# Reading the scale of every softmax exponential from a column of SBUF instead of from a register of ScalarE

## The chip, the cores and the metric

The kernel runs on one core of a Trainium2 chip. The metric is the device time of one execution in microseconds (us); lower is better. PE is TensorE, ACT is ScalarE, DVE is VectorE, POOL is GpSimd and SP is SyncE. SBUF is the on-chip memory with 128 partitions, PSUM the 8 banks into which PE writes.

## What is computed

Four layers one after another on x of shape (4, 1024, 256), all in float32, each of the form x = layernorm(x + f(x)): gated linear attention, a mixture of eight experts with top 2, differential attention, and a second mixture. The change is in the third one:

```python
# 16 heads, hd = 16, S = 1024, batch 4
q, k = x @ Wq.T + bq, x @ Wk.T + bk          # (B, H, S, 2*hd), split into q1,q2 / k1,k2, rope on each
s1 = einsum('bhqd,bhkd->bhqk', q1, k1) * scale
s2 = einsum('bhqd,bhkd->bhqk', q2, k2) * scale
a1, a2 = softmax(causal(s1)), softmax(causal(s2))
out = einsum('bhqk,bhkd->bhqd', a1 - lam * a2, v)
# rms-norm per head, times head_norm_w, then out @ Wo.T + bo
```

Each query row has a maximum subtracted ahead of the exponential, and one common factor turns the stored 16-bit scores into real ones. That factor is the value of this case.

## The kernel before, in words

The program is five stages that follow each other on every engine: `gla`, `moe`, `rope`, `attention`, `mix`. Each engine has its own instruction list in a fixed order, and the engines meet at semaphores.

`attention` runs 32 windows `w` (four batches of eight pairs of heads), and each window has 24 slots `s`. Two slots are one block of 128 keys against up to 512 queries (`span`); a block whose query range is 256 or less is done in one slot for two heads at a time (`heads_two`: slots 4, 6, 20, 22). In a slot, PE's list has in this order: the products for a row maximum of window w+2 (`maximum`, L2188 and L2193, read by DVE at L2079), the transposed scores of two of the four score maps (L2232), and weighted values of an earlier block (`products`, L2169). ACT's list has the exponentials of those scores (L1983), from a PSUM bank into the SBUF tile `E`.

The scores and exponentials go through a ring of three PSUM banks. Score i is written only after exponential i-3 has ended:

```python
if i > 2:
    e.wait_ge(S.ex, i - 2)                       # PE, ahead of the score of L2232
a = e.matmul(PS[:, singles[i % 3], c:c + n], KS[w % 4][...], QS[w % 4][...])
```

Between the exponentials ACT has a few more instructions: `out_of` (L2010, the sums of weighted values to `OT`) behind the exponentials of slot 11 and in slot 3, `put_rows` (L1961, the row maxima to `MT`) in slot 4, and `take_heads` (L2017, to `OH`) in slot 6. PE waits for each of them: the transposes of `pe_heads` (L2123, slot 5) reuse the bank that L1961 frees, and the maxima of slot 8 (L2188) reuse the bank that L2017 frees. There are 40 exponentials in a window, so 1280 in all.

The factor is the tile `SCL`, [128, 1] float32, computed by DVE in the `moe` stage (L1237) and the same in all partitions. ACT's list loads it once, at the start of `attention`, into a register of its sequencer (L1963, L1964), and every exponential names that register as its scale (L1983).

Other activations of the kernel take a scale from a [128, 1] column already: L997 and L1040 in `moe`, L1023, L1520 (both scale and bias).

Of the kernel before, what the change touches and what calls it, by code (L numbers as in the profile page):

```python
# [10 lines left out]
I32 = mybir.dt.int32  # L11
# [4 lines left out]
ACT = mybir.ActivationFunctionType  # L16
# [1676 lines left out]
def attention(nc, A, K, PS, D, own, before, keep):  # L1693
# [3 lines left out]
    S = ATT(K.banks[1])  # L1697
# [54 lines left out]
    def tail(w):  # L1752

        return (w - 9) // 8 if w >= 9 and w % 8 == 1 else None
# [42 lines left out]
    def span(m):  # L1797
        p, kt = blocks[m % 12]
        q0 = max(128 * kt, 512 * p)
        return p, kt, q0, 512 * p + 512 - q0  # L1800
# [131 lines left out]
    def roots(e, b):  # L1932
        e.wait_ge(S.ms, b + 1)
        rsqrt(e, own.act, K, MS[:], MS[:], ML[:], 1.0 / 16, 1).then_inc(S.rt, 1)

    def join_out(e, b):
        for k in HALF:
            kb, _ = turns["join", b, k]
            e.wait_ge(S.pe_pj, 2 * b + k + 1)
            e.wait_ge(S.ms, b + 1)  # L1940
            e.activation(OTT[:, k, :], flat2(kb), ACT.Copy).then_inc(S.pj, 1)

    def root4(e, b, q):
        e.wait_ge(S.mv4, 2 * b + q + 1)
        rsqrt(e, own.act, K, K.RS[:, 0:4], K.MV[:, 0:4, 1], K.LV[:, 0:4], 1.0, 0).then_inc(S.rs4, 1)

    def act(e):
        e.wait_ge(K.cleared, 2)
        e.preload_act_table_set("natural_log_exp_and_others")

        def lambdas():
            for i, (d, s) in enumerate(((L1, S.lam1), (L2, S.lam2))):
                e.wait_ge(s, (1, 2)[i])
                e.activation(d[:], d[:], ACT.Exp).then_inc(S.lamx, 1)

        def put_rows(v):
            kb, _ = turns["rows", v]
            e.wait_ge(S.pe_nm, v + 1)
            if v > 0:
                e.wait_ge(S.mlow, v)  # L1960
            e.activation(MT[:], PS[0:32, kb, 0:128], ACT.Copy, scale=-1.0 / MAXUNIT).then_inc(S.mhi, 1)  # L1961

        unit = e.alloc_register("score_unit")  # L1963
        e.reg_load(unit, K.SCL[0:1, 0:1].bitcast(I32))  # L1964

        for w in range(-2, 32):
            for s in range(24):
                if w >= 0:
                    m = 12 * w + s // 2
                    p, kt, q0, n = span(m)  # L1970
                    two = heads_two[m % 12]
                    for x in HALF if not two or s % 2 == 0 else ():
                        i = exps_to(m) + (x if two else 2 * (s % 2) + x)
                        e.wait_ge(S.pe_sc, i + 1)
                        if m >= NE:
                            e.wait_ge(S.pe_av, m - NE + 1)
                        elif i == 0:
                            before.done(e)
                        if two:
                            dst, src = E[:, m % NE, x:4:2, 0:n], PS[:, singles[i % 3], 0:2 * n].rearrange("p (y s) -> p y s", y=2)  # L1980
                        else:
                            dst, src = E[:, m % NE, 2 * (s % 2) + x, 0:n], PS[:, singles[i % 3], 0:n]
                        e.activation(dst, src, ACT.Exp, scale=unit).then_inc(S.ex, 1)  # L1983
                    if s == 11:
                        out_of(e, w, 0)
                if w >= 1 and s == 3:
                    out_of(e, w - 1, 1)
                if w >= 1 and s == 6:
                    take_heads(e, w - 1)
                if w >= 1 and s == 4 and w + 1 < 32:  # L1990
                    put_rows(w + 1)
                if w >= 8 and w % 8 == 0 and s == 23:
                    roots(e, w // 8 - 1)
                if tail(w) is not None:
                    b = tail(w)
                    if s == 9:
                        join_out(e, b)
                    if s in (14, 19):
                        root4(e, b, s // 19)
            if w < 0:  # L2000
                put_rows(w + 2)
            if w == -2:
                lambdas()
        out_of(e, 31, 1)

    def out_of(e, w, p):
        e.wait_ge(S.pe_av, 12 * w + 8 * p + 4)
        if w > 0:
            e.wait_ge(S.pe_hd, w)
        e.activation(OT[:, 512 * p:512 * p + 512], PS[:, 7, :], ACT.Copy).then_inc((S.ot0, S.ot1)[p], 1)  # L2010

    def take_heads(e, v):
        kb, _ = turns["heads", v]
        e.wait_ge(S.pe_hd, v + 1)
        if v > 1:
            e.wait_ge(S.hd, v - 1)
        e.activation(OH[v % 2][:].rearrange("p i h m d -> p (i h m) d"), flat2(kb).rearrange("p (j d) -> p j d", d=32)[:, :, 0:17], ACT.Copy).then_inc(S.ohs, 1)  # L2017
# [129 lines left out]
    def pe(e):  # L2147
# [106 lines left out]
        for s in (24, 25, 26):  # L2254
            products(372 + weighted[s][0], weighted[s][1])

    stage = namedtuple("Stage", "pe dve act pool sp")(pe, dve, act, pool, sp)
    parts = dict(S=S, M=M, OT=OT, OA=OA, CH=CH, CL=CL, ZL=ZL, room=room, turns=turns, freed=freed, exps=exps_to(384), roots=roots, join_out=join_out, root4=root4, means=means,
                 out_add=out_add, take_heads=take_heads, denominators=denominators, fetch_first=fetch_first, pe_heads=pe_heads, pe_join=pe_join, pe_out=pe_out)
# [425 lines left out]
```

## Time and profile before

| | before |
|---|---|
| median of 3 runs (lowest to highest) | 2444.31 us (2441.43 to 2449.72) |
| profiled execution: time, span | 2444.31 us, 2442.5 us |
| instructions | 50583 |
| PE busy, share of the span | 2217.5 us, 91% |
| DVE | 1581.1 us, 65% |
| ACT | 1244.2 us, 51% |
| POOL | 713.6 us, 29% |
| the exponentials of L1983 | 1280, 626.1 us busy, from 1324.7 to 2216.5 us |

The span runs from the first to the last instruction of the program that the profiler recorded, and the time has 1.8 us more. Shares are averages over five stages with different limits. An engine's record of an instruction also covers the end of its writes, so two records of the same engine can overlap: the distance from one start to the next is shorter than a record's length.

### The profile page before, as it was taken

What the parts mean: (1) busy time and instruction counts of PE and PEld (TensorE: products, weight loads), DVE (VectorE), ACT (ScalarE), POOL (GpSimd) and SP (SyncE); (2) the same over time, 40 slices, a digit from 0 to 9 for tenths busy, and PEclk for the clock granted to TensorE, in tenths of its full rate; (3) what the DMA queues carried; (4) which work ended last, traced back from release to release, by engine and by line L of the source; (5) the groups of instructions that cost most, each with busy time, mean ns of one, the idle gap of its engine ahead of it and who ended that gap; (6) DMA issues with size and microseconds to landing.
All of it is one profiled execution on the core that took longest, in us unless ns stands there. A gap on an engine that the chain in (4) does not pass through costs nothing.

```text
span 2442.5 us, 50583 instructions
## 1 busy us (share of the span) xinstructions
PE 2217.5 (91%) x17816; PEld 1367.4 (56%) x17816; DVE 1581.1 (65%) x2653; ACT 1244.2 (51%) x2537; POOL 713.6 (29%) x797
## 2 busy tenths in 40 slices
PE   7999999889999999976866999899989998999998
PEld 5777777556666666655652333333333334347887
DVE  3556666643333333338999888788878887844878
ACT  6666665213433322323322778777767876774110
POOL 1222322102333333325553232422232342223000
PEclk9999999999999999988885999999999999999999
DMA  4223334651222222232431011010001100210000
GB/s 170 87 87 103 114 113 164 207 200 32 53 36 38 38 36 38 38 98 97 164 141 41 28 48 39 30 43 33 32 25 52 37 28 28 63 37 1 18 26 27
DMA packets 89900, 164.19 MB, mean 67 GB/s; under 512 B 15952, under 2 KB 64080, under 8 KB 88000
## 3 DMA queue, kind: packets, MB, share of 16 engines
q1 hardware_dynamic: 76032, 142.20, 16.9%
q0 software_dynamic: 13632, 18.77, 4.8%
q8 instruction: 158, 2.59, 0.4%
q14 instruction: 78, 0.64, 0.1%
HBM read 99.91 MB, written 60.49 MB: 66 GB/s over the span
## 4 chain that ended last, share of the span: by engine, by line
PE 54%; DVE 11%; ACT 6%; issue 5%; DMA 2%; SPq 0%; POOL 0%; ACTq 0%; DVEq 0%
PE PS L2169 10%; PE PS L1404 8%; PE PS L58 6%; PE PS L60 6%; PE PS L59 6%; PE PS L2232 6%; PE PS L2193 4%; ACT E L1983 4%; DVE NM L2079 3%; PE PS L2188 2%; PE PS L1389 2%; DVE X L2416 2%; DVE TT L1597 2%; PE PS L2123 1%; PE PS L2144 1%
## 5 line engine op out<-in xcount | busy, mean ns | idle before, releaser
L2079 DVE TENSOR_REDUCE NM<-PS 128x2 f32<-128x1024 f32 (+3 forms) x608 | 679.9, 1160 | 138.2 <-PE PS L2193 131.9
L1983 ACT ACTIVATE E<-PS 128x512 f32<-128x512 f32 (+2 forms) x1280 | 626.1, 560 | 206.7 <-PE PS L2232 194.9
L2169 PE MATMUL PS<-E,VP 128*32 128x256 f32 (+1 forms) x5120 | 370.8, 371 | 0.5 <-ACT OT L2010 0.5
L1916 POOL TENSOR_SCALAR_AFFINE_SELECT E<-E 128x512 f32<-128x512 f32 x256 | 162.5, 635 | 411.7 <-ACT E L1983 411.6
L1201 DVE SCALAR_TENSOR_TENSOR XIL<-PS,XSC,XIH 128x128 f16<-128x128 f32 x142 | 43.2, 346 | 335.4 <-ACT XIH L997 335.4
L2232 PE MATMUL PS<-QK 50*128 50x512 f16 (+3 forms) x1152 | 214.2, 329 | 16.2 <-ACT E L1983 16.0
L1032 ACT ACTIVATE HB<-PS 128x768 f32<-128x768 f32 x71 | 57.6, 811 | 300.8 <-PE PS L1389 300.8
L2169 PEld LDWEIGHTS PS<-E,VP 128*32 128x32 f32 x5120 | 108.4, 109 | 161.0 <-issue 117.3
L1404 PE MATMUL PS<-WALL,HB 128*128 x852 | 195.7, 379 | 1.0 <-ACT HB L1032 1.0
L2193 PE MATMUL PS<-QK 48*128 48x512 f16 (+3 forms) x1152 | 180.6, 344 | 9.6 <-DVE NM L2079 9.0
L941 POOL DMA_INDIRECT XB<-x_normed,IDX x71 | 71.1, 1001 | 364.9 <-DVE GAT L1217 315.5
L58 PE MATMUL PS<-WALL,XIH 128*128 x426 | 162.2, 381 | 6.9 <-issue 5.5
L1404 PEld LDWEIGHTS PS<-WALL,HB 128*128 128x128 f32 x852 | 156.5, 190 | 20.7 <-issue 2.4
L59 PE MATMUL PS<-WALL,XIH 128*128 x426 | 162.1, 381 | 0.0
L60 PE MATMUL PS<-WALL,XIL 128*128 x426 | 162.0, 380 | 0.0
L2416 DVE SCALAR_TENSOR_TENSOR X<-PS,COMB,X 128x256 f32<-128x256 f32 x256 | 123.6, 483 | 23.2 <-PE PS L60 15.4
L2232 PEld LDWEIGHTS PS<-QK 50*128 50x128 f16 x1152 | 85.8, 94 | 91.5 <-ACT E L1983 53.8
L2188 PE MATMUL PS<-MR 64*128 64x64 bf16 (+2 forms) x1408 | 93.1, 211 | 43.2 <-DVE NM L2079 24.5
L1510 POOL TENSOR_TENSOR TT<-TT 128x512 f32<-128x512 f32 x64 | 105.2, 1643 | 91.7 <-DVE TT L1597 90.8
L2188 PEld LDWEIGHTS PS<-MR 64*128 64x128 bf16 x1408 | 41.4, 95 | 161.8 <-issue 75.5
L932 POOL DMA_INDIRECT x_resid<-YI,IDX x71 | 112.7, 1588 | 37.4 <-issue 19.7
L80 ACT ACTIVATE LV<-MV,EPS 128x4 f32<-128x4 f32 (+1 forms) x43 | 12.7, 296 | 184.2 <-DVE MV L74 140.8
(347 smaller groups left out, 4178.6 us busy)
## 6 DMA issues: line engine op xcount, KB each, us to landing
parts<-PP SPq DMA_DIRECT2D x32, 512.0 KB, 3.0
WIN<-in_we SPq DMA_DIRECT2D x16, 768.0 KB, 5.2
QK<-parts SPq DMA_DIRECT2D x96, 128.0 KB
WALL<-pairs_of_weights SPq DMA_DIRECT2D x7, 1536.0 KB
pairs_of_weights<-WPH SPq DMA_DIRECT2D x16, 384.0 KB, 2.3
pairs_of_weights<-WPL SPq DMA_DIRECT2D x16, 384.0 KB, 3.2
WALL<-in_we SPq DMA_DIRECT2D x8, 768.0 KB
QK<-parts SPq DMA_DIRECT2D x96, 64.0 KB
```

Of the source, the lines that this page charges most:

```text
L58: e.matmul(o, lh, rh, start=start, stop=False)
L59: e.matmul(o, lh, rl, start=False, stop=False)
L60: return e.matmul(o, ll, rh, start=False, stop=stop)
L1404: a = e.matmul(PS[:, b1 + 2, 0:256], HT[:, i, :], wide(r_last, 3072 + 256 * i, 256), start=i == 0, stop=i == 5)
L1916: e.affine_select(out=E[:, m % NE, :, 0:128], in_=E[:, m % NE, :, 0:128], pattern=[[0, 4], [1, 128]], compare_op=ALU.is_ge, fill=0.0, base ...
L1983: e.activation(dst, src, ACT.Exp, scale=unit).then_inc(S.ex, 1)
L2079: e.tensor_reduce(dst, src, AX, ALU.max).then_inc(S.mx, 1)
L2169: a = e.matmul(PS[32 * jj:32 * jj + 32, 7, 512 - n + c0:512 - n + c1], VP[b % 2][:, kt, 17 * hd:17 * hd + 32], E[:, m % NE, jj, c0:c1], st ...
L2188: e.matmul(PS[:, kb + x, 0:n * len(parts)].rearrange("p (z s) -> p z s", s=n)[:, :, c:c + 64], places[h][r, :], later[r, :].unsqueeze(1).t ...
L2193: a = e.matmul(PS[:, kb + x, n * z:n * z + n], q[r, y, 128 * i:128 * i + 128], k[r, y, c0:c0 + n], start=not masked, stop=True, skip_group ...
L2232: a = e.matmul(PS[:, singles[i % 3], c:c + n], KS[w % 4][r, y, 128 * kt:128 * kt + 128], QS[w % 4][r, y, q0:q0 + n], start=True, stop=True)
L2416: a = e.scalar_tensor_tensor(out=X[:, t, :], in0=PS[:, product_bank(g), 256 * j:256 * j + 256], scalar=COMB[:, t, 2 * ep + j:2 * ep + j + ...
```

## The change

The register and its load go. The scale of each exponential becomes the column `K.SCL[:]`, one value for each partition, which ACT reads from SBUF. The value is the same, nothing is added to or taken from any engine's list but the one load, and no semaphore changes.

```diff
-        unit = e.alloc_register("score_unit")
-        e.reg_load(unit, K.SCL[0:1, 0:1].bitcast(I32))
-
         for w in range(-2, 32):
             for s in range(24):
...
-                        e.activation(dst, src, ACT.Exp, scale=unit).then_inc(S.ex, 1)
+                        e.activation(dst, src, ACT.Exp, scale=K.SCL[:]).then_inc(S.ex, 1)
```

## Rows read from the trace of the kernel before

**Rows 1.** Windows: `attention`, seven regular periods, the two beside a batch's end, the last three.

```profile
core 0: us, PE busy (x) PEld busy (x) DVE busy (x) ACT busy (x) POOL busy (x), PEclk, DMA share, GB/s
1356.03:1539.12 183.09, 172.17 (x2163) 67.48 (x2164) 150.94 (x148) 146.31 (x308) 55.01 (x98) 1.00 0.12 39
1539.12:1606.82 67.70, 58.76 (x666) 27.55 (x667) 53.85 (x70) 45.38 (x96) 24.88 (x44) 1.00 0.07 25
2139.37:2217.60 78.23, 75.87 (x745) 33.35 (x747) 28.00 (x35) 56.67 (x119) 21.64 (x38) 1.00 0.09 29
```

**Rows 2.** Groups of ACT by shape: count, busy us, mean ns, idle before.

```profile
L1983 ACT ACTIVATE E<-PS 128x512 f32<-128x512 f32 x896 | 472.9, 605 | 92.4 <-PE PS L2232 85.3
...
L2010 ACT ACTIVATE OT<-PS 128x512 f32<-128x512 f32 x64 | 38.9, 607 | 1.2 <-PE PS L2169 1.2
...
L1040 ACT ACTIVATE SI<-PS,UN 128x768 f32<-128x768 f32 x71 | 64.0, 902 | 0.5 <-PE PS L60 0.5
L1032 ACT ACTIVATE HB<-PS 128x768 f32<-128x768 f32 x71 | 57.6, 811 | 300.8 <-PE PS L1389 300.8
L997 ACT ACTIVATE XIH<-PS,XSC 128x128 f16<-128x128 f32 x142 | 44.5, 364 | 65.1 <-PE PS L1363 65.1
L354 ACT ACTIVATE SQ<-PS 128x128 f32<-128x128 f32 x112 | 31.1, 278 | 22.4 <-PE PS L671 10.6 <-ACT SQ L354 0.4
L1520 ACT ACTIVATE X<-X,NMR,RS 128x256 f32<-128x256 f32 x32 | 16.6, 589 | 26.4 <-DVE NMR L1571 26.4
```

**Rows 3.** Timeline of ACT in `moe` and `rope`: start, length, merged neighbours.

```profile
670.40 0.90 ACT L1040 ACTIVATE SI<-PS,UN 128x768 f32<-128x768 f32 x1
671.18 1.15 ACT L1023 ACTIVATE CS<-CS,CQ 128x1024 f32<-128x1024 f32 x1
...
1086.02 2.07 ACT L1520 ACTIVATE X<-X,NMR,RS 128x256 f32<-128x256 f32 x4 [0.23 <-DVE NMR L1571]
```

**Rows 4.** Timeline of ACT over one regular period.

```profile
1462.23 0.66 ACT L1983 ACTIVATE E<-PS 128x256 f32<-128x256 f32 x2 [1.62 <-PE PS L2232]
1462.77 0.63 ACT L2017 ACTIVATE OH<-PS 128x544 f32<-128x544 f32 x1
1464.16 2.07 ACT L1983 ACTIVATE E<-PS 128x512 f32<-128x512 f32 x4 [0.76 <-PE PS L2232]
1466.40 2.10 ACT L1983 ACTIVATE E<-PS 128x512 f32<-128x512 f32 x4 [0.18 <-PE PS L2232]
1468.39 0.60 ACT L2010 ACTIVATE OT<-PS 128x512 f32<-128x512 f32 x1
1468.87 7.43 ACT L1983 ACTIVATE E<-PS 128x512 f32<-128x512 f32 x14
...
1484.31 0.87 ACT L1983 ACTIVATE E<-PS 128x384 f32<-128x384 f32 x2 [0.20 <-PE PS L2232]
1485.07 0.60 ACT L2010 ACTIVATE OT<-PS 128x512 f32<-128x512 f32 x1
...
1486.50 0.26 ACT L1961 ACTIVATE MT<-PS 32x128 f32<-32x128 f32 x1
```

**Rows 5.** Timeline of PE over the same period, scores and waits.

```profile
1463.46 0.23 PE L2188 MATMUL PS<-MR 64*128 64x64 bf16 x4 [0.26 <-ACT OH L2017]
...
1469.54 0.39 PE L2232 MATMUL PS<-QK 50*128 50x512 f16 x1 [0.31 <-ACT E L1983]
...
1471.77 0.38 PE L2232 MATMUL PS<-QK 50*128 50x512 f16 x2
1472.88 0.38 PE L2232 MATMUL PS<-QK 50*128 50x512 f16 x2
1473.76 0.57 PE L2232 MATMUL PS<-QK 50*128 50x512 f16 x2
...
1484.86 0.49 PE L2232 MATMUL PS<-QK 50*128 50x256 f16 x3 [0.41 <-ACT E L1983]
...
1486.82 1.09 PE L2123 MATMUL PS<-IDN,OT 128*128 128x128 f32 x8 [0.36 <-ACT MT L1961]
```

## The prediction

> **What bounds the kernel now.** I read the windows of `attention` first, because every instruction that the change touches lies there [rows 1]. Seven regular windows of the loop take 183.09 us, 26.16 us each, with PE busy 172.17 us (94%), DVE 82% and ACT 80% at a granted clock of 1.00. So PE sets the end of this stage, and `mix` begins where it ends; what PE loses here is lost to the kernel. ACT has 5.3 us idle in each window. That number tempts one to call a dearer exponential free, so the next question is where in the window this idle time lies, and whether PE waits for ACT at the same time.
>
> The timelines of one regular period answer it [rows 4, 5]. ACT is idle ahead of a few exponentials (1.62, 0.76, 0.18, 0.20 us), but from 1466.40 to 1476 us it runs nearly without a pause: 4 exponentials, the copy of L2010, then 14 exponentials in 7.43 us. PE waits for ACT four times in the period: 0.26 us for L2017, 0.31 and 0.41 us for an exponential, 0.36 us for L1961. The two engines are coupled closely. The ring of three PSUM banks lets PE be only three scores ahead, so the second score of each slot waits for the first exponential of the slot before.
>
> **The change part by part.**
>
> *The register load that goes.* One instruction of ACT's sequencer at the start of the stage, where ACT's next instruction waits for the first row maxima of PE and DVE, which cover it. It happens once, against 1280 exponentials: 0 both ways.
>
> *The form with a register.* Does it cost anything now that would come back? The exponential of 512 columns takes 605 ns with the register, the copy of 512 columns with an immediate scale 607 ns, both from PSUM to SBUF [rows 2]. From start to start it is the same too: L2010 starts at 1485.07 and L1961 at 1486.50, with two exponentials between, so 0.477 us for each of the three steps; L2010 alone is followed after 0.48 us (1468.39, 1468.87) [rows 4]. Nothing comes back.
>
> *The column as scale.* The trace has this form on other lines. L1040 (scale column, 768 columns, PSUM) takes 902 ns, and L1032 (no column, same shape) 811: 91 ns more. L997 against L354 (128 columns, PSUM): 364 against 278, 86 ns. The question that matters more is whether the added time also stands between starts, or lies under the instruction before. L1520 has two columns: four of them take 2.07 us with 589 ns each, so (2.07 - 0.59) / 3 = 0.494 us from start to start at 256 columns [rows 2, 3]. Two exponentials of 256 columns take 1462.77 - 1462.23 = 0.54, 0.27 each [rows 4]. Difference 0.224 for two columns, 0.112 for one, and part of it may be the SBUF source. So it is not hidden. L1040 confirms it: the next one starts 0.78 us after it, for 768 columns, where 512 plain columns need 0.477; at the slope of (811 - 607) / 256 = 0.80 ns a column 768 plain ones would need 0.68, so 0.10. Bounds 0.086 and 0.112; I take 0.091, the row of the nearest kind (PSUM source, one column, over 500 columns). By these numbers ACT gets 1280 x 0.091 = 116 us more work. In a window that is 40 x 0.091 = 3.6 us, less than its 5.3 us of idle time, so ACT does not become the bound on average. Its bursts decide.
>
> The Trainium skill (ScalarE: Activation LUTs, "What ACT_TABLE_LOAD costs") gives about 93 ns for each pointer operand, and says that activations in a row overlap by about 93 ns. The rows agree on the first; on the second they show 605 - 477 = 128 ns. With its overlap an exponential with a column would start every 605 ns and not every 568; worked out from that page as an estimate, the same bursts would cost about 1 us more in a window and the kernel would come to some 2505 us. I stay with the rows.
>
> *What PE loses in one period*, followed slot by slot with exponentials of 512 columns at 0.568 from start to start and 0.69 long (384 columns: 0.38 + 0.09), PE resuming 0.05 after the end it waits for, as now [rows 4, 5]:
> 1. Two exponentials precede L2017 at 1462.77: it starts and ends 0.18 later, and PE at 1463.46 is waiting for it: +0.17.
> 2. The four exponentials from 1464.16 and the first of the next four fall behind by 0.09 each. The second scores of slots 9 to 12, which already wait for an exponential, move to +0.26, +0.26, +0.34, +0.47.
> 3. L2010 (1468.39) starts after four exponentials that began 0.26 late: +0.54. The exponential behind it is the one that PE waits for at 1469.54: +0.54 + 0.09, so +0.62.
> 4. The 14 exponentials from 1468.87. PE's slots 15 and 16 come 1.11 us apart (1471.77, 1472.88), a pair on ACT now needs 1.14: +0.02 to 0.03 each. The next slot comes after 0.88, must now be stretched, and its second score, late by 0.18 already, gets later: +0.75.
> 5. Slots 18 to 22 with 384, 256 and 128 columns hold this: +0.75, and +0.83 at the two-headed block of slot 20.
> 6. From the new window's slot 1 its second score again: +0.91. Slots 2 and 3 hold. At slot 4 the score that waits 0.41 us (1484.86) is at +0.99.
> 7. ACT then runs without a pause: L2010 (1485.07) at +1.09, two exponentials, and L1961 (1486.50) at +1.09 + 0.18 = +1.27. PE's transposes at 1486.82 wait for it: +1.27.
>
> So a period goes from 26.16 to 27.43 us. DVE and POOL wait for PE and ACT in between and move with them; POOL's masks (L1916) are read by PE two or more slots later and are covered. SP issues nothing from this line: its fetches are three windows ahead. The same steps give 1.7 us a period at 0.112, 1.1 at 0.086, and 0.5 at 0.05.
>
> *The sum.* There are 22 regular periods: 22 x 1.27 = 27.9. Beside the end of each batch two periods take 67.70 us, with DVE on the path for parts of them [rows 1]; the bursts there are the same up to slot 22, after it ACT has pauses. Estimate 1.2 for the shorter and 0.9 for the longer one, three times: 6.3. The first window is slow already (31.3 us from the first exponential to 1356.03), with PE slower and ACT in less of a hurry: 0.5. The last 78.23 us hold nearly three windows, two of them without maxima, where ACT paces PE in the slots without other matmuls and PE's matrix products cover the rest [rows 1]: 1.3 for the first, 0.9 and 1.2 for the others, 3.4. Sum 38.1, over the profiled execution's 2444.31 us (span 2442.5 and 1.8 around it), which is also the median of the three runs: 2482.
>
> **The rivals.**
>
> *Hidden read, no change.* ACT fetches the column while the instruction before still runs, or while it waits for its score. For it: 5.3 us of idle time a window [rows 1]. Against it: the spacing of L1520 and L1040 [rows 3]. Time 2444. Chance 7%.
>
> *Part of it absorbed.* The price is 0.05 instead of 0.09 because this source, function or place in the queue hides some, or PE makes up its lateness in waits for DVE that I let move along. For it: PE's busy time stays at 24.6 us a window, so 1.5 us are waits of one kind or another. By 0.5 to 0.9 us a window, 15 to 27 us in all: 2459 to 2471. Chance 15%.
>
> *More than ACT's own chain.* PE's share falls from 94% to 24.6 / 27.43 = 90%, and the granted clock drops in places; or the price is that of the L1520 rows. The ends of the batches have PE at 58.76 / 67.70 = 87% with a clock of 1.00 in the first of them [rows 1], which speaks against a drop. With 0.112, 2482 + 22 x 0.43 + 3 = 2494; with some periods at a lower clock, 2495 to 2515. Chance 14%.
>
> *Faster.* The register has a price that the lengths don't show: the sequencer must have it ready ahead of every exponential, and this stands in the spacing. It would decide if the steps between exponentials shrank by 0.02 us or more, column included; PE's four waits for ACT, 1.34 us a period, are the most to be had: 32 x 1.34 = 43 us, so 2401 to 2435. Against it: 0.477 and 0.48 from start to start with and without the register. Chance 3%.
>
> **How the numbers follow.** The forecast, the sum above, has 61%: 2482, with a range of its own from 2471 to 2494. The range of 8 in 10 takes in the upper half of the absorbed case and a part of the dearer one: 2463 to 2497. A change of 0.3%, 7.3 us, is about what a measurement of this kernel can tell from none. Slower by more has the forecast, the absorbed case and the dearer one, 0.90; within it the hidden read, 0.07; faster 0.03.
>
> **What the changed profile would show.** The exponentials of 512 columns at 696 ns in the groups, L1983 at some 742 us in total and ACT near 1360. Two of them in a row 0.57 us apart. L2123 every 27.4 us in place of 26.16. PE's waits for L1983, L2017 and L1961 longer (about 2.6 us a period in place of 1.34), and its waits for DVE (L2079) not longer. If the exponentials are longer but the period is not, the step on the bursts is wrong; if their length is 605, the price is. Clock values below 1.00 in the regular periods would point to the dearer rival. `mix` and the stages ahead must be unchanged.

## The result and the profile after

The changed kernel takes 2509.34 us (median of 4 runs, 2502.47 to 2510.5), the kernel before 2446.28 (4 runs, 2441.43 to 2449.72). The ratio is 1.025, with a 95% interval of 1.0228 to 1.0273: 63 us slower, where 38 were forecast and 2497 was the upper end of the range.

First the length of the instructions that changed, in the groups of ACT by shape (count, busy us, mean ns, idle before). L1980 is the exponential, which was L1983.

```profile
L1980 ACT ACTIVATE E<-PS,SCL 128x512 f32<-128x512 f32 x896 | 541.0, 701 | 75.2 <-PE PS L2229 74.6
...
L1040 ACT ACTIVATE SI<-PS,UN 128x768 f32<-128x768 f32 x71 | 64.0, 901 | 0.5 <-PE PS L60 0.5
...
L2007 ACT ACTIVATE OT<-PS 128x512 f32<-128x512 f32 x64 | 38.9, 608 | 1.2 <-PE PS L2166 1.2
```

The exponential of 512 columns went from 605 to 701 ns [rows 2], 96 ns; the lines that the change does not touch stayed. Next one regular window, first ACT's timeline and then PE's scores and waits. The window begins at PE's transposes of 1502.36, which answer to those of 1486.82 - 26.16 = 1460.66 in the kernel before, so 41.70 is to be subtracted for a comparison with [rows 4] and [rows 5].

```profile
1503.93 0.84 ACT L1980 ACTIVATE E<-PS,SCL 128x256 f32<-128x256 f32 x2 [1.63 <-PE PS L2229]
1504.66 0.62 ACT L2014 ACTIVATE OH<-PS 128x544 f32<-128x544 f32 x1
1506.04 4.75 ACT L1980 ACTIVATE E<-PS,SCL 128x512 f32<-128x512 f32 x8 [0.76 <-PE PS L2229]
1510.66 0.61 ACT L2007 ACTIVATE OT<-PS 128x512 f32<-128x512 f32 x1
1511.14 10.28 ACT L1980 ACTIVATE E<-PS,SCL 128x512 f32<-128x512 f32 x18
...
1528.07 0.60 ACT L2007 ACTIVATE OT<-PS 128x512 f32<-128x512 f32 x1
1528.55 1.27 ACT L1980 ACTIVATE E<-PS,SCL 128x512 f32<-128x512 f32 x2
1529.68 0.25 ACT L1961 ACTIVATE MT<-PS 32x128 f32<-32x128 f32 x1
```

```profile
1505.34 0.23 PE L2185 MATMUL PS<-MR 64*128 64x64 bf16 x4 [0.44 <-ACT OH L2014]
...
1511.91 0.39 PE L2229 MATMUL PS<-QK 50*128 50x512 f16 x1 [0.68 <-ACT E L1980]
...
1513.03 0.42 PE L2229 MATMUL PS<-QK 50*128 50x512 f16 x2
...
1514.18 0.43 PE L2229 MATMUL PS<-QK 50*128 50x512 f16 x2
...
1515.34 0.42 PE L2229 MATMUL PS<-QK 50*128 50x512 f16 x2
...
1516.27 0.65 PE L2229 MATMUL PS<-QK 50*128 50x512 f16 x2
...
1527.76 0.49 PE L2229 MATMUL PS<-QS,KS 50*128 50x256 f16 x3 [0.29 <-ACT E L1980]
...
1529.99 1.09 PE L2120 MATMUL PS<-IDN,OT 128*128 128x128 f32 x8 [0.63 <-ACT MT L1961]
```

A merged row names the shape of its first instruction: the 18 exponentials from 1511.14 are 14 of 512 columns and 4 of 384, which the kernel before has in two rows with a pause of 0.18 us between them. From 1506.04 to the end of these 18 (1521.42) ACT now has no pause. PE waits 0.44, 0.68, 0.29 and 0.63 us where it waited 0.26, 0.31, 0.41 and 0.36, and some of its pairs of scores are drawn out by waits that the merged rows show only as a longer pair (0.65 at 1516.27). The window is 27.63 us long, against 26.16. Between starts the exponential costs as much more as the prediction took: the two from 1528.55 stand (1529.68 - 1528.55) / 2 = 0.565 us apart, where 0.568 was forecast. The same two in the kernel before have (1486.50 - 1485.55) / 2 = 0.475:

```profile
1485.55 1.10 ACT L1983 ACTIVATE E<-PS 128x512 f32<-128x512 f32 x2
```

But not every window is. From transposes to transposes:

```profile
core 0: us, PE busy (x), PEclk, DMA share, GB/s
1418.07:1445.69 27.62, 25.38 (x309) 1.00 0.26 74
1445.69:1474.73 29.04, 26.81 (x309) 0.94 0.08 29
1474.73:1502.36 27.63, 25.38 (x310) 1.00 0.09 31
1454.00:1457.00 3.00, 2.32 (x24) 0.95 0.26 94
1457.00:1460.00 3.00, 3.00 (x22) 0.50 0.12 49
1510.67:1513.67 3.00, 2.32 (x28) 1.00 0.25 98
1513.67:1516.67 3.00, 3.00 (x34) 1.00 0.13 53
```

A *low stretch* here is a time in which the granted clock is 0.50. The second window, with one in it, is 1.42 us longer, with the same matmuls and a mean granted clock of 0.94. The two rows from 1454.00 on look into it: from 1457 to 1460 the clock is 0.50 (1.2 GHz), and in the 3 us before, PE was busy only 2.32 us, because the score wait of 0.68 us lies there. The last two rows are the same place in the undisturbed window above, with the same 2.32 us and the same wait, and the clock stays at 1.00: the wait alone does not tell which window is hit. So two things happened: every window got 1.47 us longer, and some got a stretch at the lower clock as well.

### The profile page after: what moved, and what is told of

Its sections match the earlier page's. It is cut to its first block, busy times and chain, and to the rows that moved or that the text cites. A ratio compares the mean times of both kernels' runs of the same rounds, so it can differ in the third digit from the quotient of the medians.

```text
span 2499.4 us, 50582 instructions
## 1 busy us (share of the span) xinstructions
PE 2256.3 (90%) x17816; PEld 1382.2 (55%) x17816; DVE 1585.5 (63%) x2653; ACT 1338.1 (54%) x2537; POOL 713.4 (29%) x797
## 4 chain that ended last, share of the span: by engine, by line
PE 55%; DVE 10%; ACT 6%; issue 5%; DMA 2%; SPq 1%; POOL 0%; ACTq 0%; DVEq 0%
PE PS L2166 11%; PE PS L1404 7%; PE PS L2229 7%; PE PS L58 6%; PE PS L60 6%; PE PS L59 6%; PE PS L2190 4%; ACT E L1980 4%; DVE NM L2076 3%; PE PS L2185 2%; PE PS L1389 2%; DVE TT L1597 2%; PE PS L2120 2%; DVE X L2413 1%; PE PS L2141 1%
## 5 line engine op out<-in xcount | busy, mean ns | idle before, releaser
L1980 ACT ACTIVATE E<-PS,SCL 128x512 f32<-128x512 f32 (+2 forms) x1280 | 721.2, 657 | 171.0 <-PE PS L2229 170.0
L2166 PE MATMUL PS<-E,VP 128*32 128x256 f32 (+1 forms) x5120 | 376.8, 376 | 0.5 <-ACT OT L2007 0.5
L2229 PE MATMUL PS<-QK 50*128 50x512 f16 (+3 forms) x1152 | 235.9, 335 | 26.2 <-ACT E L1980 21.5
L2229 PEld LDWEIGHTS PS<-QK 50*128 50x128 f16 x1152 | 92.7, 95 | 130.1 <-ACT E L1980 105.4
```

The lines of the kernel that those rows point to most:

```text
L1980: e.activation(dst, src, ACT.Exp, scale=K.SCL[:]).then_inc(S.ex, 1)
L2166: a = e.matmul(PS[32 * jj:32 * jj + 32, 7, 512 - n + c0:512 - n + c1], VP[b % 2][:, kt, 17 * hd:17 * hd + 32], E[:, m % NE, jj, c0:c1], st ...
L2229: a = e.matmul(PS[:, singles[i % 3], c:c + n], KS[w % 4][r, y, 128 * kt:128 * kt + 128], QS[w % 4][r, y, q0:q0 + n], start=True, stop=True)
```

## The experiments

Each run stood beside runs of the kernel before on the same chip (medians 2446.6, 2448.4 and 2449.0 in the three sets). "Undisturbed window" below means a regular window with a granted clock of 1.00 throughout.

**1. Half of the exponentials with a column: the wide blocks.** Against the kernel before:

```diff
-  e.activation(dst, src, ACT.Exp, scale=unit)
+  e.activation(dst, src, ACT.Exp, scale=K.SCL[:] if n == 512 else unit)
```

> The column is the scale of the 28 exponentials of a window whose block has 512 queries (slots 0, 1 and 8 to 17), the register that of the other 12. Theory (what counts is where a longer exponential stands in front of a wait of PE): the steps of slots 9 to 17 and slot 1 stay, those of slots 4 and 6 (L1961, L2017) go, so about 0.8 us a regular window, 27 us in all, and a few us of clock more: 2470 to 2482. Rival (each column costs its share, wherever it stands): 28/40 of the 63 us, so 2490.

The expectation counted wrongly: blocks of 256 queries are done for two heads in one instruction of 512 columns, so the column is on 24 of the 40 and the register on 16; the rival by count becomes 24/40 x 63 = 38 us, 2484.

Measured: 2485.8 us (6 runs, 2476.3 to 2504.7), ratio 1.0173 (1.014 to 1.0206), 4 us over the expected range and near the corrected rival. The undisturbed window is 27.01 us, +0.85 (0.8 was expected). Four regular windows have a low stretch, the first among them:

```profile
core 0: us, PE busy (x), PEclk, DMA share, GB/s
1358.17:1386.57 28.40, 26.61 (x309) 0.94 0.09 30
1413.67:1440.68 27.01, 25.22 (x309) 1.00 0.27 75
```

**2. The other half: the narrow blocks.** Against the kernel before:

```diff
-  e.activation(dst, src, ACT.Exp, scale=unit)
+  e.activation(dst, src, ACT.Exp, scale=unit if n == 512 else K.SCL[:])
```

> The column only on the 12 exponentials of a window that belong to blocks of 384, 256 and 128 queries (slots 2 to 4, 6, 18 to 20, 22), the register on the rest. Theory: 0.18 in slot 6 ahead of L2017, and in slots 2 to 4 some 0.4 ahead of L1961, 0.6 us a window, 19 us in all with little clock: 2463 to 2470. Rival by count: 12/40 of 63 = 19 us, 2465. This one does not tell the two apart; with the run of the wide blocks it says whether the two halves add up to the whole.

Measured: 2483.2 us (2478.1 to 2491.8), ratio 1.0144 (1.0118 to 1.0171), 13 us over the expected range. The undisturbed window is 26.78, +0.62, as expected. Its windows, in a row:

```profile
core 0: us, PE busy (x), PEclk, DMA share, GB/s
1357.02:1383.81 26.79, 24.83 (x310) 1.00 0.10 32
1383.81:1411.65 27.84, 26.29 (x309) 0.94 0.09 31
1411.65:1438.43 26.78, 24.93 (x309) 1.00 0.28 76
```

In the first batch the second, fourth and sixth window have a low stretch and are 1.06 us longer; it begins 0.2 us behind the start of the transposes, which end the longest wait of this run's window, about 0.6 us for L1961:

```profile
1383.81 1.78 PE L2123 MATMUL PS<-IDN,OT 128*128 128x128 f32 x8 [0.60 <-ACT MT L1961]
```

The two halves' undisturbed windows add up to 0.85 + 0.62 = 1.47, the whole's 1.47. The times do not add up: 39 + 37 = 76 against 63. The surplus of 13 us is in the clock: the medians of the runs' mean clocks are 0.957 and 0.952, against 0.962 beside them and 0.953 for the changed kernel, and 0.01 of it goes with 18 us (below). On the rival by count this pair is silent, since 1.47 x 24/40 = 0.88 and x 16/40 = 0.59.

**3 and 4. ACT's copies ahead of the exponentials**, with the column and with the register.

```diff
         for w in range(-2, 32):
             for s in range(24):
+                if w >= 1 and s == 6:
+                    take_heads(e, w - 1)
+                if w >= 1 and s == 4 and w + 1 < 32:
+                    put_rows(w + 1)
                 if w >= 0:
...
-                if w >= 1 and s == 6:
-                    take_heads(e, w - 1)
-                if w >= 1 and s == 4 and w + 1 < 32:
-                    put_rows(w + 1)
```

> The changed kernel, but ACT does L1961 ahead of the exponentials of slot 4 and the copy to OH ahead of those of slot 6. PE waits 0.63 and 0.44 us for these two in a window of the changed kernel, and they carry 0.5 us of the 1.47 that a window lost. Theory: both waits go, 30 x 1.07 = 32 us less, and with shorter pauses of PE some of the stretches at a clock of 0.5 go as well (up to 12 us): 2465 to 2477. Rival: the loss is ACT's busy time, and the waits turn up at the scores behind: less than 10 us gained, 2500 or more.

> The kernel before with the same order of ACT's list. PE waits 0.36 and 0.26 us for the two copies in a window. Theory: 30 x 0.62 = 19 us less, 2427. Rival: the score waits of 0.31 and 0.41 us or those for DVE (DVE is 82% busy) take most of it: 2438 to 2446.

Measured with the column: 2487.0 us (2483.6 to 2494.1), ratio 1.0159 (1.0134 to 1.0184), 22 us less than the changed kernel where 32 and more were expected, and more than twice what the rival (ACT's busy time is the loss) allowed. With the register: 2433.2 us (2430.4 to 2439.4), ratio 0.9945 (0.9922 to 0.9969), faster than both kernels of this case, by 13 us where 19 were expected. Seven windows of the latter take 178.52 us, 25.50 each, 0.66 less than before, as expected; the median of its runs' mean clocks is 0.959 against 0.962 beside it, which at 18 us per 0.01 is about the 6 us that are missing:

```profile
1354.33:1532.85 178.52, 171.90 (x2168) 67.35 (x2164) 150.94 (x148) 146.84 (x309) 55.29 (x99) 1.00 0.13 40
```

The windows of the column's version show why its gain is smaller than its windows promise:

```profile
core 0: us, PE busy (x), PEclk, DMA share, GB/s
1389.55:1417.40 27.85, 26.67 (x313) 0.94 0.09 31
1417.40:1443.84 26.44, 25.26 (x314) 1.00 0.28 77
1443.84:1471.71 27.87, 26.69 (x314) 0.94 0.09 30
```

An undisturbed window is 26.44, so the early copies gave 1.19 us where 1.07 were expected, and the column costs only about 0.9 more than the register in the same order. But 12 of the 22 regular windows now have a low stretch that begins in them, most of them 1.4 us longer at 0.94, and three have one three times as long (30.4 us at 0.83). The low stretches begin 9 to 10 us into a window, behind the same long score wait of slot 13:

```profile
1398.63 0.42 PE L2229 MATMUL PS<-QK 50*128 50x512 f16 x1 [0.68 <-ACT E L1984]
```

**5. A constant in place of the register.** Against the kernel before:

```diff
-        unit = e.alloc_register("score_unit")
-        e.reg_load(unit, K.SCL[0:1, 0:1].bitcast(I32))
...
-  e.activation(dst, src, ACT.Exp, scale=unit)
+  e.activation(dst, src, ACT.Exp, scale=1e-10)
```

> The scale of the exponentials is a constant in the instruction, 1e-10 (so the softmax is computed with another temperature), neither register nor column; the register load is gone. Theory (the register costs what a constant costs): 600 to 605 ns for 512 columns, regular windows of 26.16 us, same time as before, 2440 to 2452. Rival (the register has a price of its own, so that part of what the column costs was paid before): shorter steps between exponentials, and 2438 or less.

Measured: 2448.3 us (12 runs, 2440.4 to 2451.3), ratio 0.9999 (0.9986 to 1.0011). The 512-column form takes 605 ns and the regular window 26.16, to the digit the values with the register.

```profile
L1980 ACT ACTIVATE E<-PS 128x512 f32<-128x512 f32 x896 | 473.0, 605 | 94.3 <-PE PS L2229 87.1
```

**6. A second column.** Against the changed kernel:

```diff
-  e.activation(dst, src, ACT.Exp, scale=K.SCL[:])
+  e.activation(dst, src, ACT.Exp, bias=K.EPS[:, 3:4], scale=K.SCL[:])
```

> The changed kernel with a second column, a bias of 1e-28 for each exponential, which changes no result by more than that. Theory: the price per column is 0.096 on ACT and adds up, 793 ns for 512 columns; by the same slot-by-slot steps a window now is bound by ACT nearly throughout and loses 4.5 us against before in place of 1.47, three times as much and not twice: 32 x 3.0 = 96 us over the changed kernel, 2590 to 2620. Rival (loss in proportion to the added time): 63 us more, 2572.

Measured: 2624.3 us (5 runs, 2620.7 to 2628.8), ratio 1.0732 (1.0711 to 1.0752). That is 115 us over the changed kernel, where 96 were expected, and 4 us over the expected range; nearly every window has low stretches (the runs' mean clock is 0.930 to 0.935). The groups of ACT, and the one regular window without a low stretch (busy PE, PEld, DVE, ACT, POOL):

```profile
L1980 ACT ACTIVATE E<-PS,EPS,SCL 128x512 f32<-128x512 f32 x896 | 626.8, 797 | 79.1 <-PE PS L2229 78.6
```

```profile
2030.59:2061.22 30.63, 27.50 (x310) 10.26 (x310) 22.17 (x21) 27.09 (x44) 7.84 (x14) 1.00 0.08 28
```

797 - 701 = 96 ns again, so the price per column is the same for the second. The window went from 26.16 to 27.63 to 30.63: +1.47, then +3.00. The slot-by-slot steps had 4.5 in all and got 4.47. That rejects a loss in proportion to the added time (2572 was its forecast). ACT's idle time in a window shows where the difference went: 5.26 us before, 27.63 - 23.73 = 3.90 in the changed kernel's window from 1502.36, 30.63 - 27.09 = 3.54 with two. The first column used up 1.36 us of it and the second 0.36.

**7 and 8. More matmuls in front of PE's waits**, with the column three times (shown, against the changed kernel) and with the register twice.

```diff
-            for z, (i, y, c0, n) in enumerate(parts):
+            for z, (i, y, c0, n) in [(z, part) for _ in range(3 if s in (5, 13) else 1) for z, part in enumerate(parts)]:
```

> The changed kernel; PE writes the row-maximum products of slots 5 and 13 three times in place of once (same values, same bank), 0.44 us more matmuls in front of each of its two longest waits for ACT (0.63 and 0.68 us). ACT's path is untouched. Theory (some 20 of the 63 us are stretches at the granted clock of 0.5, which come where PE's pauses lie): windows without such a stretch stay at 27.63 to 27.7 us, the extra stretches mostly go, clock 0.96 or more, 2485 to 2498. Rival (the low clock has nothing to do with PE's pauses): clock stays at 0.953 to 0.958, 2502 to 2512; and if the extra products lie on the path after all, 2520 and more.

> The control of the run before: the kernel before with the products of slots 5 and 13 twice, 0.22 us more in front of waits of 0.36 and 0.31 us. Its regular windows have hardly any low clock to lose. Both theories: 2438 to 2450, clock 0.96 to 0.97. 2455 and more would say that the extra products are not hidden, in both kernels.

Measured with the column: 2496.1 us (5 runs, 2489.2 to 2504.9), ratio 1.0199 (1.0174 to 1.0225): 13 us faster than the changed kernel, by doing more work; the two intervals (1.0228 to 1.0273 for the changed kernel) just do not touch. The control with the register: 2445.5 us (12 runs, 2440.5 to 2458.2), ratio 0.9999 (0.9982 to 1.0016), no change, so the added matmuls are hidden. Seven windows of the column's run, and its waits:

```profile
core 0: us, PE busy (x), PEclk, DMA share, GB/s
1361.08:1554.45 193.37, 183.38 (x2219) 1.00 0.11 37
```

```profile
1507.42 0.82 PE L2190 MATMUL PS<-QK 48*128 48x512 f16 x6
1508.76 0.39 PE L2229 MATMUL PS<-QK 50*128 50x512 f16 x1 [0.30 <-ACT E L1980]
...
1526.83 1.09 PE L2120 MATMUL PS<-IDN,OT 128*128 128x128 f32 x8 [0.20 <-ACT MT L1961]
```

193.37 / 7 = 27.62 us, the same undisturbed window as in the changed kernel: what ACT costs is untouched. The waits are 0.30 and 0.20 in place of 0.68 and 0.63, and no window of the seven has any low clock; of the 22 regular windows one has, and that stretch began in the batch's end before it (1864.18:1893.15, 28.97 us at 0.93). The median of the runs' clocks rose from 0.953 to 0.961.

**9. The early copies and the filled wait of slot 13 together**, with the column. The diff is that of run 3 and that of run 7 with slot 13 alone.

> The run with the column and the early copies, and the products of slot 13 three times as in the filled run (0.44 us of matmuls in front of a score wait of about 0.7 us). Its regular windows have come down to 26.43 us, but over 100 us of the stage have the granted clock of 0.5, always beginning 9 to 10 us into a window, in and behind slot 13, and it stands at 2487. Theory (the early copies' gain is half eaten by the low clock that follows PE's wait in slot 13): regular windows of 26.4 to 26.5 us without low stretches, clock 0.955 or more, 2462 to 2475. Rival (the low clock comes from the sum of the pauses over a window, not from this place): clock stays near 0.95, 2483 to 2490.

Measured: 2460.3 us (6 runs, 2457.8 to 2466.2), ratio 1.0049 (1.0033 to 1.0066), 27 us faster than run 3 and 2 us under the expected range.

```profile
core 0: us, PE busy (x), PEclk, DMA share, GB/s
1386.80:1413.26 26.46, 25.67 (x317) 1.00 0.10 33
```

The windows are those of run 3 without its disturbed half; no regular window has a low stretch. The rival, that the sum of the pauses decides and not this place, forecast 2483 to 2490 and is rejected by the time. The filled wait shortens the sum too, so the windows say it better: PE's pauses add up to 26.44 - 25.26 = 1.18 us in an undisturbed window of run 3, and 12 of its 22 regular windows are hit; in the kernel before they add up to 1.56 us, with no wait longer than 0.41, and no regular window is hit.

## Why the prediction came out as it did

**The direction and the mechanism held.** PE is the bound, ACT's average idle time does not cover its bursts, and the loss comes out of the places that were named. Seven steps were forecast for one window; this is the changed window against them (start minus 41.70, against [rows 4, 5]):

| step | forecast | measured |
|---|---|---|
| L2017, now L2014, and PE behind it | +0.17 | 1505.34: +0.18 |
| L2010 in slot 11 (1468.39), now L2007 | +0.54 | 1510.66: +0.57 |
| score wait of slot 13 (1469.54) | +0.62 | 1511.91: +0.67 |
| second score of slot 17 | +0.75 | 1516.27 + 0.65 - 0.39 = 1516.53: +0.89 |
| score wait of slot 4 (1484.86) | +0.99 | 1527.76: +1.20 |
| L1961 (1486.50) | +1.27 | 1529.68: +1.48 |

**The price of a column** was right: 0.091 was taken, within the bounds 0.086 and 0.112. The length grew by 0.096, and the distance between starts, where nothing else holds ACT up, by 0.565 - 0.475 = 0.09. Its double in run 6 and the equal length of register and constant in run 5 show that this is the whole price.

**Step 4, the burst**, was the largest error of the window. It took 1.14 us for a pair of exponentials. Measured, PE's slots 14 to 16 in this burst (1513.03, 1514.18, 1515.34) stand about 1.16 apart in place of 1.11. So each slot added 0.04 to 0.05 and not 0.02 to 0.03. At the 0.565 from above a pair would need 1.13 on ACT, so its pace alone does not give the 1.16; what does, no run shows. Of the 0.20 to 0.21 us by which the window was underestimated, 0.05 were there before this step, 0.09 came in it and 0.07 between slot 17 and slot 4. Over 22 windows that is 4.4 us.

**The step that failed is the one that put the clock into a rival at 14%.** It was named there ("the granted clock drops in places"), and spoken against with a row in which PE was busy 87% with a clock of 1.00. The average over 68 us does not carry this, and the row was the mild one of three. The ends of the second and third batch of the kernel before have low stretches, 3.4 and 6.8 us of them, at the same share of PE busy (87%):

```profile
core 0: us, PE busy (x), PEclk, DMA share, GB/s
1763.76:1832.53 68.77, 60.03 (x666) 0.98 0.07 25
1989.46:2059.81 70.35, 61.53 (x666) 0.95 0.07 24
```

So the sum put the clock at nothing, although the trace of before had it in this stage. What the runs show is local: a wait of 0.68 us in a stretch with 2.32 of 3 us busy is followed by 3 us at 0.50, in one regular window of each of the first three batches in the changed kernel's profile. One such stretch costs 1.42 us. Runs 7 and 9 remove them by filling the wait and leave ACT's part as it is; they gain 13 and 27 us. Runs 2 and 3 have more of them than the changed kernel, with no more work on ACT. Across repeated runs of one kernel the same is seen: run 1 took 2476.3 us at a mean clock of 0.964 and 2504.7 at 0.948, so 18 us for each 0.01. The changed kernel's runs have 0.953 to 0.958, those of the kernel before 0.957 to 0.967. With medians of 0.953 and 0.962, about 16 of the 63 us are the clock's and 47 the longer windows'; 32 x 1.47 = 47 says the same by another way. The rival's range for this case, 2495 to 2515, holds the measured 2509.

**The sum, term by term**, for the profiled executions, whose spans differ by 2499.4 - 2442.5 = 56.9 us (the median run took some 8 us more than this one, at a clock of 0.953 against 0.958):

| term | forecast | measured |
|---|---|---|
| 22 regular windows | 27.9 | 35.8 (of it 4.3 in three low stretches; 0.9 less because one wait for a DMA of before is covered) |
| six windows at the ends of batches | 6.3 | 10.7 (27 us of low stretches in place of 10) |
| the first window | 0.5 | 3.7 (13 us in place of 7.5) |
| the last three | 3.4 | 6.8 (7 us in place of 0) |
| start of the stage later | 0 | 3.1 |
| from the last transposes to the end | 0 | -3.2 |
| sum | 38.1 | 56.9 |

The terms for the first window and the batch ends were estimates without a slot-by-slot count. The ends of the three batches in the changed kernel, and the whole last part, again with low stretches in it, are in these rows:

```profile
core 0: us, PE busy (x), PEclk, DMA share, GB/s
1557.61:1629.25 71.64, 62.22 (x666) 0.95 0.07 24
1796.54:1868.18 71.64, 62.22 (x667) 0.95 0.07 24
2035.38:2109.61 74.23, 64.89 (x667) 0.91 0.07 23
```

```profile
2192.67:2278.94 86.27, 82.35 (x762) 36.07 (x763) 27.92 (x35) 66.56 (x121) 21.63 (x38) 0.96 0.08 26
```

In all, this stage has 39 us more of low stretches than before, of which 10 lie in regular windows and 17 at batch ends. At 0.4 us lost for each us of them (1.42 for a stretch of 3.4 us; an estimate for the other places) they are some 16 of the 56.9 us. Without them the windows sum to about 41 where 38.1 was forecast. That the rest comes out so close is in part luck: by the same estimate the regular windows were put 4 us too low and the batch ends 2 too high.

That the stage starts 3.1 us later is not shown to be the change's doing: the first exponential came at 1327.9 in the changed kernel's profile, at 1324.7 in that of before, and at 1326.7 in that of run 5, which has the time of before. Ahead of it lie 144, 136 and 146 us of low stretches in these three.

**The other rivals.** *Hidden read*: rejected, the spacing grew with the length (0.475 to 0.565). *Part absorbed*: rejected, the undisturbed window lost more than forecast. *Faster, because the register has a price*: rejected by run 5. The reading of the Trainium skill that gave some 2505 us by another overlap between activations (ScalarE: Activation LUTs, "What ACT_TABLE_LOAD costs") came nearer to the time, but not for its reason. With it an exponential with a column would start every 701 - 93 = 608 ns; the rows have L2007 at 1510.66 and, eight exponentials earlier, 1506.04, so (1510.66 - 1506.04) / 8 = 578 ns, some of it PE's pace, and 565 for the two from 1528.55. Its 93 ns for a pointer operand agree with the 96 measured.

**What stays open.** Where exactly the clock falls depends on how PE's waits lie in time, and which windows are hit repeats in a pattern that the runs show but do not explain. It was not tried whether the same trick helps at the batch ends, where most of the remaining low stretches of runs 4, 7 and 9 lie. In the batch-end windows no run separates ACT's share from the clock's, and why slots 14 to 16 stand 1.16 us apart is open.

## What to carry to other kernels

An operand that adds a tenth of a microsecond to an instruction is free only if the burst in which it stands has room, and not if the engine has idle time on average; take one period and carry the lateness from wait to wait. If a scalar is the same in all partitions and goes into a thousand activations, take a register or a constant, which cost the same here; a column cost 96 ns more each time. When TensorE waits for another engine, look at the granted clock of single windows of the loop: hoisting the small copies that others wait for gained 13 us on the kernel before. Where low stretches follow a wait, matmuls that write the same values again, put into that wait, gained 13 and 27 us here with ACT's path as it was; where there were none to remove (run 8), they gained nothing.

## What the runs showed of the hardware that was not expected

- More matmuls made the kernel faster: 0.88 us of repeated row-maximum products a window, in front of waits, took 2509 to 2496 us (run 7), and half of that took 2487 to 2460 (run 9).
- The granted clock went to 0.50, 1.2 GHz, for a stretch behind 3 us in which PE had been busy for 2.32 us and waited once, for 0.68 us. In other windows the same 3 us were not followed by it.
- Which windows are hit follows a pattern of its own (every second one in the first batch of run 2, one in a batch of the changed kernel), so a smaller loss in each window can cost as much: runs 1 and 2 lost 39 and 37 us with 0.85 and 0.62 us a window.
- A scale from a register costs ACT the same as a constant, 605 ns for 512 columns; a column costs 96 ns and a second column 96 ns more.
